# Moving the small triangular substitution of a chunked delta-rule kernel from VectorE to GpSimd

## What is computed

```python
def step(S, inp):
    q_t, k_t, v_t, a_t, b_t = inp
    kS = jnp.einsum('bhd,bhdv->bhv', k_t, S)
    kkS = jnp.einsum('bhd,bhv->bhdv', k_t, kS)
    S = a_t[..., None, None] * (S - b_t[..., None, None] * kkS) + jnp.einsum('bhd,bhv->bhdv', k_t, v_t)
    o_t = jnp.einsum('bhdv,bhd->bhv', S, q_t)
    return (S, o_t)
...
q = _causal_conv_silu(x @ Wq.T, conv_q).reshape(Bx, Tx, H, DK)
k = _causal_conv_silu(x @ Wk.T, conv_k).reshape(Bx, Tx, H, DK)
v = _causal_conv_silu(x @ Wv.T, conv_v).reshape(Bx, Tx, H, DV)
q = _l2_norm(q)
k = _l2_norm(k)
alpha = jnp.exp(-jnp.exp(A_log) * jax.nn.softplus(a_lin + dt_bias))
beta = 2.0 * jax.nn.sigmoid(x @ Wb.T)
o, _S = _gdn_recurrence(q.astype(jnp.float32), k.astype(jnp.float32), v.astype(jnp.float32), alpha, beta)
o = _rms_norm(o).astype(x.dtype).reshape(Bx, Tx, H * DV)
return o @ Wo.T
```

## Time and profile before

| what | value |
|---|---|
| median of 3 runs | 4844.67 us (4843.56 to 4845.88) |
| profiled execution, its time | 4845.65 us |
| its span, first to last instruction | 4843.8 us |
| PE busy | 4096.6 us, 85% |
| VectorE busy | 3575.8 us, 74% |
| ScalarE busy | 2828.8 us, 58% |
| GpSimd busy | 1312.3 us, 27% |
| mean granted TensorE clock | 0.970 |

### The profile page before, as it was taken

How to read it: one execution, slowest core, us unless ns; L and a number is a source line. 1 busy time by engine, 2 the same in 40 slices (tenths; PEclk the granted TensorE clock), 3 DMA queues, 4 the chain that set the end, 5 groups by cost and what they waited for, 6 DMA issues and landing times. The chain is left out here.

```text
span 4843.8 us, 155608 instructions
## 1 busy us (share of the span) xinstructions
PE 4096.6 (85%) x59788; PEld 2913.1 (60%) x59788; DVE 3575.8 (74%) x8216; ACT 2828.8 (58%) x4519; POOL 1312.3 (27%) x1318
## 2 busy tenths in 40 slices
PE   5888888888888888888888888888888888888855
PEld 4666665666666665666666666666656666665644
DVE  5777777777777777777777777777777777777745
ACT  2566656565565656556565655666565556656534
POOL 2222222222222222222222222222222222222211
PEclk9999999999999999999999999999999999999977
DMA  1211111111111111121111111111111111111111
GB/s 52 43 37 41 39 37 41 38 42 38 42 37 38 41 37 42 38 42 37 39 40 36 41 38 42 37 40 39 37 41 38 42 38 41 38 37 41 37 39 40
DMA packets 877985, 191.77 MB, mean 40 GB/s; under 512 B 816000, under 2 KB 873600, under 8 KB 877952
## 3 DMA queue, kind: packets, MB, share of 16 engines
q1 hardware_dynamic: 871648, 173.49, 17.1%
q0 software_dynamic: 6304, 17.84, 1.3%
HBM read 136.16 MB, written 55.06 MB: 39 GB/s over the span
## 5 line engine op out<-in xcount | busy, mean ns | idle before, releaser
L826 DVE SCALAR_TENSOR_TENSOR cv<-ps,w_v,cv 128x512 f32<-128x512 f32 x768 | 576.7, 751 | 553.3 <-ACT cv L691 535.1
L826 DVE SCALAR_TENSOR_TENSOR cv<-ps,w_kq,cv 128x512 f32<-128x512 f32 x768 | 574.4, 748 | 87.5 <-ACT cv L691 69.3
L607 PE MATMUL ps<-QG,S 64*128 64x64 f32 x4096 | 431.7, 274 | 3.3
L610 PE MATMUL ps<-PT,U 64*128 64x64 f32 x4096 | 429.2, 272 | 0.0
L458 PE MATMUL ps<-Lm,k_all 128*128 128x512 f32 x768 | 419.3, 627 | 0.0
L691 ACT ACTIVATE cv<-ps,w_kq 128x512 f32<-128x512 f32 x256 | 175.9, 687 | 399.2 <-PE ps L447 399.2
L1002 POOL TENSOR_TENSOR qn<-sl,sq 128x512 f32<-128x512 f32 x128 | 161.8, 1264 | 906.2 <-ACT sq L729 906.2
L467 PE MATMUL ps<-sq,k_all 128*128 128x512 f32 x512 | 287.6, 644 | 125.9 <-ACT ex L698 125.8
L706 ACT ACTIVATE sl<-cv 128x512 f32<-128x512 f32 x256 | 161.3, 630 | 395.1 <-DVE cv L826 395.1
L447 PE MATMUL ps<-xnT,w_v 128*128 (+1 forms) x1024 | 296.2, 410 | 97.0 <-DVE Nd L841 53.0
L607 PEld LDWEIGHTS ps<-QG,S 64*128 64x128 f32 x4096 | 342.5, 188 | 30.5 <-issue 30.5
(11 more groups left out here) (183 smaller groups left out, 10441.2 us busy)
## 6 DMA issues: line engine op xcount, KB each, us to landing
scrN<-Nd SPq DMA_DIRECT2D x256, 128.0 KB, 2.4
Z<-scrZ SPq DMA_DIRECT2D x256, 128.0 KB, 2.9
X<-scrX SPq DMA_DIRECT2D x512, 64.0 KB, 2.6
w_v<-wtab SPq DMA_DIRECT2D x128, 132.0 KB, 2.2
w_kq<-wtab POOLq DMA_DIRECT2D x128, 132.0 KB, 2.4
wo_s<-wo SPq DMA_DIRECT2D x128, 128.0 KB, 2.4
NS<-scrN SPq DMA_DIRECT2D x128, 64.0 KB, 2.6
scrZ<-XT SPq DMA_DIRECT2D x128, 64.0 KB, 2.5
```

The costliest lines, as they stand in the source:

```text
L607: nc.tensor.matmul(o_cols(h, b), unit(S, b)[a:z], sub_block(BD["QG"], 0, b, a, z), start=True, stop=False)
L610: last = nc.tensor.matmul(o_cols(h, b), unit(U, b)[a:z], sub_block(BD["PT"], 0, b, a, z), start=False, stop=True)
L826: nc.vector.scalar_tensor_tensor(cv4[:, j], pj[:, :, k:k + C], tap(j, k), cv4[:, j], ALU.mult, ALU.add).then_inc(conv.sem, 1)
```

## The change

The 8x8 blocks are now inverted by columns on GpSimd (`pool_elim`, 14 instructions in a row, semaphore `elim`): a copy that sets `XT` to the identity again, a copy of the first column, and six pairs of a product into a new buffer `tmpE` and a sum onto `XT`, on 14 to 32 elements per partition. It stands at the end of GpSimd's body, behind `QG`. `dve_sub` keeps the five instructions that join the blocks (`SUBS = 5`), and its first one waits for `elim`. In `dve_body` both halves of the update of S now stand ahead of it.

```diff
-SUBS = 18
+ELIM = 14
+SUBS = 5
...
+        def pool_elim(pool, n):
+
+            if not first(n):
+                pool.wait_ge(z_out.sem, z_out.at(n - 1))
+                pool.wait_ge(sub.sem, sub.at(n - 1))
+            pool.sem_inc(pool_go.sem, 1)
+            nc.gpsimd.tensor_copy(XT[0:64, 0:256], k_all[0:64, K_XI:K_XI + 256]).then_inc(elim.sem, 1)
+            pool.wait_ge(n_in.sem, n_in.at(n))
+            for k in range(7):
+                r, c = 7 - k, k + 1
+                pool.wait_ge(elim.sem, elim.at(n, max(2 * k, 1)))
+                if k == 0:
+                    pool.sem_inc(pool_go.sem, 1)
+                    nc.gpsimd.tensor_copy(XB8[:, :, 0, 1:8], NB8[:, :, 1:8, 0]).then_inc(elim.sem, 1)
+                else:
+                    t = tmpE[0:64, 0:2 * r * c].rearrange("g (u j i) -> g u j i", u=2, j=c)
+                    nc.gpsimd.tensor_tensor(t, NB8[:, :, c:8, k:c].rearrange("g u i o -> g u o i").to_broadcast([64, 2, c, r]),
+                                            XB8[:, :, 0:c, k:c].to_broadcast([64, 2, c, r]), ALU.mult).then_inc(elim.sem, 1)
+                    pool.wait_ge(elim.sem, elim.at(n, 2 * k + 1))
+                    nc.gpsimd.tensor_tensor(XB8[:, :, 0:c, c:8], XB8[:, :, 0:c, c:8], t, ALU.add).then_inc(elim.sem, 1)
...
             for k in range(lo, hi):
                 if k == 0:
                     dve.wait_ge(n_in.sem, n_in.at(n))
-                    if not first(n):
-                        dve.wait_ge(z_out.sem, z_out.at(n - 1))
-                    dve.wait_ge(c_in.sem, C_IN)
-                    ins = nc.vector.tensor_scalar(XB8[:, :, 0, 1:2], NB8[:, :, 1, 0:1], 0.0, None, ALU.add)
+                    dve.wait_ge(elim.sem, elim.at(n))
+                    ins = nc.vector.tensor_tensor(prod, N16[:, 8:16, 0:8].rearrange("g a (o b) -> g a o b", o=1).to_broadcast([64, 8, 8, 8]),
+                                                  X16[:, 0:8, 0:8].rearrange("g (o c) b -> g o c b", o=1).to_broadcast([64, 8, 8, 8]), ALU.mult)
...
@@ dve_body @@
                 dve_conv(dve, n, 3)
-                dve_sub(dve, n, 0, 10)
             if m is not None:
                 dve_s(dve, m, 0)
-            if n is not None:
-                dve_sub(dve, n, 10, 14)
-            if m is not None:
                 dve_s(dve, m, 1)
             if n is not None:
-                dve_sub(dve, n, 14, 15)
+                dve_sub(dve, n, 0, 2)
             if m is not None:
                 dve_on(dve, m)
             if n is not None:
-                dve_sub(dve, n, 15, 17)
+                dve_sub(dve, n, 2, 4)
                 dve_p(dve, n)
-                dve_sub(dve, n, 17, SUBS)
+                dve_sub(dve, n, 4, SUBS)
                 dve_k(dve, n)
@@ pool_body @@
                 pool_prepare(pool, m, n)
+                pool_elim(pool, n)
```

More of the change, by code:

```diff
@@ L119, in build @@
         tmpW = sb("tmpW", 64)
+        tmpE = sb("tmpE", 32)
         scrN = nc.dram_tensor("scrN", (NB * SB,), F32, kind="Internal").ap()
@@ L363, in build @@
         n_in = sig("n_in", 16)
+        elim = sig("elim", ELIM)
+        pool_go = sig("pool_go", 2)
         sub = sig("sub", SUBS)
@@ L869, in dve_sub @@
                     dve.wait_ge(n_in.sem, n_in.at(n))
-                    if not first(n):
-                        dve.wait_ge(z_out.sem, z_out.at(n - 1))
-                    dve.wait_ge(c_in.sem, C_IN)
-                    ins = nc.vector.tensor_scalar(XB8[:, :, 0, 1:2], NB8[:, :, 1, 0:1], 0.0, None, ALU.add)
+                    dve.wait_ge(elim.sem, elim.at(n))
+                    ins = nc.vector.tensor_tensor(prod, N16[:, 8:16, 0:8].rearrange("g a (o b) -> g a o b", o=1).to_broadcast([64, 8, 8, 8]),
+                                                  X16[:, 0:8, 0:8].rearrange("g (o c) b -> g o c b", o=1).to_broadcast([64, 8, 8, 8]), ALU.mult)
                 else:
                     dve.wait_ge(sub.sem, sub.at(n, k))
[L876 to L887, removed]
+                if k == 1:
                     ins = nc.vector.tensor_reduce(WT.rearrange("g c a -> g a c"), prod, AX, ALU.add)
-                elif k == 15:
+                elif k == 2:
                     ins = nc.vector.tensor_tensor(prod, X16[:, 8:16, 8:16].rearrange("g (o b) a -> g a o b", o=1).to_broadcast([64, 8, 8, 8]),
                                                   WT.rearrange("g (o c) b -> g o c b", o=1).to_broadcast([64, 8, 8, 8]), ALU.mult)
-                elif k == 17:
+                elif k == 3:
+                    ins = nc.vector.tensor_reduce(X16[:, 0:8, 8:16].rearrange("g c a -> g a c"), prod, AX, ALU.add)
+                elif k == 4:
                     if not first(n):
@@ L895, in dve_sub @@
                     ins = nc.vector.tensor_copy(XB[0:64, :].rearrange("g (j k) -> g j k", j=16), X16.rearrange("g k j -> g j k"))
-                elif k == 16:
-                    ins = nc.vector.tensor_reduce(X16[:, 0:8, 8:16].rearrange("g c a -> g a c"), prod, AX, ALU.add)
                 ins.then_inc(sub.sem, 1)
```

## The result

The changed kernel takes 4916.07 us (median of 4 runs, 4913.96 to 4925.14), the kernel before 4845.01 us (median of 4, 4843.56 to 4845.88, run beside it): 1.49% slower, ratio 1.0149 with a 95% interval of 1.0136 to 1.0162, or 71 us. The forecast was 4930, the range 4800 to 5100.

A forecast was written before the change was run, and what follows sets the result against it. A step was taken as one loop of waits through `on`, the next step's front part, output matmuls and QG. Late `on` 60, clock 23 and 2 more make 85 us on 4845.65: forecast 4930, range 4800 to 5100.

The forecast's parts named there:

- The point from which it decides: The period stays if VectorE can start the join 4.11 us after QG's end; join start to `on` needs 1.30 us.
- The term of 60 us: `on` starts 0.47 us late in each step (4.58 us against 4.11), x 127 = 60 us.
- Nothing gives it back: From `on` on, every engine keeps the same instructions in the same order, so the 0.47 us a step stays lost.
- The chain on GpSimd: From QG's end to the join: 14 instructions with pauses and the hop to VectorE, 4.58 us in sum.
- reset: GpSimd's copy of XT, 256 elements, at the start of the chain: 0.45 us, between 0.39 and 0.69.
- hop: From the end of GpSimd's chain to VectorE: 0.06 us, estimated from pauses.
- The much slower rival: A small two-input instruction on GpSimd costs 0.37 us, twice VectorE's: 2.1 us late a step, 5205 us; chance 0.10.
- The clock: TensorE's longer idling makes its clock fall in half of the steps instead of a third: 0.18 us a step, 23 us.
- The weights: The issue of w_kq moves behind the elimination; with 1.2 us of cover it costs nothing.
- Both ways into the next step go through the start of `on`: VectorE's queue and TensorE's both pass the start of `on`; moving it against QG moves the period by the same amount.
- Faster: Rival: GpSimd's small instructions cost less, chain 3.65 us, 0.46 less than 4.11; 4777 us, chance 0.18.
- What is removed: Thirteen small instructions off VectorE; the time counts only if `on` comes earlier; S can begin near 2407.

The follow-up runs named there:

- the early reset: The changed kernel with the copy that resets XT moved into an idle stretch of GpSimd, ahead of the wait for the query norm: 4868.09 us.
- the projection first: Old and changed kernel, each with the next step's first projection ahead of the transposes of V on TensorE and weights requested earlier: 4781.99 and 4839.44 us.

## Why the prediction was right

*The point from which it decides* (4.11 us from QG's end to the join) held: `on` started 1.32 us behind the join against 1.30 assumed, and from the kernel before to the changed one and the early reset the short step follows `on` to within 0.1 us (34.9, 35.3, 34.7 for 5.41, 5.84, 5.28). The term of 60 us came out as 42: `on` is 0.43 us late against 0.47, and the short step grew by only 0.34 of it. "Nothing gives it back" was wrong by these 0.09 us, the earlier start of Lm shown above. With the projection first in both kernels Lm starts 4.96 and 4.98 us behind `on`, and there the one-to-one rule holds: `on` is 0.46 us later and the step 0.47 longer. The point says when the change turns good, and the early reset crosses it: 5.28 against 5.41, short steps of 34.7 us.

*The chain on GpSimd.* Forecast 4.58 us, measured 4.52. Term by term: reset 0.45 against 0.39; first column 0.19 and its pause 0.17, both met; twelve products and sums 2.79 against 2.85; their twelve pauses 0.96, met at 0.08 each; hop 0.06 against 0.03. The groups of GpSimd by shape show the largest:

```profile
L886 POOL TENSOR_TENSOR tmpE<-NS,XT 64x30 f32<-64x30 f32 x256 | 64.9, 254 | 20.0
L889 POOL TENSOR_TENSOR XT<-XT,tmpE 64x30 f32<-64x30 f32 x256 | 61.1, 239 | 20.1
```

A start cost and a slope from two sizes sixteen and more times larger gave 0.24 us for 30 elements; 0.25 and 0.24 it is. The much slower rival, twice VectorE's 0.18, fell with it, and so did its rule for such sizes: the Trainium skill's factor of two (GPSIMD Engine Reference, section 4.1) is 1.3 to 1.4 here (254 and 239 ns for 30 elements against 183 for 32), 1.8 at 512.

*The clock.* Forecast 0.18 us a step, 23 us, by half of the steps instead of a third having a fall. Measured 0.20 us, 25 us: 62% of the steps are long, but the long ones last 0.86 us more than the short ones on average, not 1.06; in the step shown the fall comes only in the middle of the projection. These are two errors of opposite sign, so it is luck that the size came out. In the total, 72 us instead of 85, the chain has 18 us less than forecast, the clock 2 more, and the first step and the two ends 3 more. The larger error is in the reason given: I took the added idling for the cause and mentioned that L500 moves only in passing. The early reset starts `on` earlier than the old kernel and still has 94 long steps; with the transposes put back, 31. The move of L500, a consequence of the new place of S, made most of them there; that it did so in the changed kernel is inferred from this.

*The weights.* Covered, as said, but with some 0.5 us of room instead of 1.2: the transfer's issue starts 0.74 us behind the chain, and with 2.4 us to landing it is there at 2480.6, while the projection can start 2.26 us behind `on`, at 2481.1. Ahead of the loop it follows the chain at once. That the branch of the loop, formerly run while QG was at work, lies there is argued from this and was not tested. TensorE waits 14.0 us for `w_kq` against 7.1 before: one wait of 4.50 us in step 1 and one of 2.40 us in the single step of 39.4 us were added. The three steps of 37.2 us have none; their granted clock averages 0.91.

*What the prediction had wrong about the loop.* "Both ways into the next step go through the start of `on`": there is a third, ScalarE's silu, that ends together with `on`. It did not matter for a change that makes `on` later; it decides for one that makes it earlier. By these ends *Faster*, as priced (0.46 us a step), could not have come in full, which no run tested, and silu kept TensorE idling when `on` was put ahead of the join; the time that this order took off a step was lost in falls of the clock.

*What is removed.* As said: 13 instructions off VectorE turned into 2.65 us of waiting for GpSimd and a longer wait for TensorE (3.77 us). The start of S was guessed at 2407, near QG's release; it stands 0.99 us behind it, which made no difference.

## What to carry to other kernels

Work moved to an engine that idles is free only if its result is there when the first engine used to be ready, not when the idle engine has time: count from the last input of the moved work to its first consumer, and put it ahead of work that nobody waits for (QG, NM) rather than behind it. The same 14 instructions cost 57 us behind QG and came with a gain of 199 us ahead of NM, over the old kernel with the same help.

On a kernel whose TensorE clock comes and goes, read the lengths of all steps, not their mean: a shift of small matmuls into or out of an idle stretch moved this one by 52 us with no distance on the critical way changed.

Two engines that release the same instruction within 0.1 us look like one in the waits of a trace. Before moving the one that is shown, look where the other ends.

## What the runs showed of the hardware beyond expectation

- A wait added to TensorE made the kernel 52 us faster (4868.09 to 4815.83), by splitting 2.32 us of idling; with the projection drawn into the stretch instead, the clock fell in none of the old kernel's 126 loop steps and in one of the changed kernel's.
- In the run with four more products the clock was at 0.50 for transposes and projection in the step shown and no step kept the full clock: 62 us on top of 160 us of chain.
- A product on VectorE with both inputs in SBUF grew from 0.68 to 1.79 us beside QG (elimination between NM and QG), and QG from 1.27 to 1.96 us beside such a product (the whole join ahead of `on`); sums of S, with one input in PSUM, kept 2.15 us beside the elimination.
- A copy of 16 elements a partition on VectorE takes 0.16 us by itself and 0.53 or 0.63 us when it starts beside GpSimd's Lm, with its end 0.03 us behind Lm's. That the two exclude each other there is inferred from these ends.
